# Row maxima of a two-head side: both heads in the two halves of TensorE's array, from the high parts alone, with VectorE adding the masks

## The reference, cut to what matters

```python
def _attn(q, k, v, mask=None):
    s = jnp.einsum('bhqd,bhkd->bhqk', q, k) / np.float32(np.sqrt(HD))
    if mask is not None:
        s = jnp.where(mask, s, jnp.float32(-1000000000.0))
    return jnp.einsum('bhqk,bhkd->bhqd', jax.nn.softmax(s, -1), v)
...
o1 = _attn(q, k1, v1, causal[None, None])
...
o2 = _attn(q, ks, vs)
...
winmask = causal & (ii[:, None] - ii[None, :] < WINDOW)
o3 = _attn(q, kw, vw, winmask[None, None])
```

## Time and profile before

| | |
|---|---|
| three runs, us | 3157.45, 3162.90, 3165.65 (median 3162.9) |
| the profiled execution, us | 3156.08 |
| its span, us | 3154.3 |
| mean granted TensorE clock | 0.923 of full |
| busy share over the span | TensorE matmul 86%, VectorE 58%, ScalarE 44%, GpSimd 20% |
| TensorE busy in the slices of the attention part | nine tenths or more in nearly all |

### The profile page before, as it was taken

The page is one execution under the profiler, slowest core; times in us unless marked ns, Lnnn a source line. Parts: engine busy times, 40 slices in busy tenths (PEclk is TensorE's granted clock), DMA queues, the critical chain, the costliest instruction groups (busy, mean ns, idle before and its releaser), DMA issues. The chain is left out here.

```text
span 3154.3 us, 48599 instructions
## 1 busy us (share of the span) xinstructions
PE 2699.1 (86%) x17280; PEld 1719.6 (55%) x17280; DVE 1818.9 (58%) x3117; ACT 1373.8 (44%) x2816; POOL 634.7 (20%) x607
## 2 busy tenths in 40 slices
PE   5666575763999997999997999998999994999999
PEld 3544344442555554555654655554555552777777
DVE  4746656484466555456555556655646644667655
ACT  2333233230444543544543545543545453555544
POOL 0322405042011001001101001101101102445445
PEclk9787878785999998999998999999999996999999
DMA  2542617068655464555554455654554512000000
GB/s 85 196 159 104 251 47 304 24 246 218 127 107 120 108 124 96 114 125 120 108 114 106 106 121 114 130 115 96 124 116 98 121 33 87 18 17 3 20 10 7
DMA packets 191886, 342.32 MB, mean 109 GB/s; under 512 B 65632, under 2 KB 95040, under 8 KB 191152
## 3 DMA queue, kind: packets, MB, share of 16 engines
q1 hardware_dynamic: 191664, 339.49, 42.6%
HBM read 224.56 MB, written 112.99 MB: 107 GB/s over the span
## 5 line engine op out<-in xcount | busy, mean ns | idle before, releaser
L1340 ACT ACTIVATE prob<-ps 128x512 f32<-128x512 f32 (+5 forms) x1600 | 645.2, 441 | 903.1 <-PE ps L1291 828.3
L1393 DVE TENSOR_REDUCE maxima<-ps 128x1 f32<-128x512 f32 (+3 forms) x768 | 387.4, 547 | 352.3 <-PE ps L1222 181.3
L1312 PE MATMUL ps<-prob,plain 128*32 128x512 f32 (+5 forms) x3200 | 587.5, 449 | 0.0
L1363 POOL TENSOR_TENSOR products<-products,sums 128x256 f32<-128x256 f32 x192 | 140.5, 732 | 1695.2 <-DVE sums L1384 1694.0
L1398 DVE TENSOR_REDUCE maxima<-ps 128x2 f32<-128x512 f32 (+1 forms) x512 | 297.5, 611 | 271.4 <-PE ps L1240 129.9
L1384 DVE RECIPROCAL sums<-sums 128x256 f32<-128x256 f32 x192 | 331.6, 1736 | 96.8 <-ACT sums L1351 96.8
L1312 PE MATMUL ps<-prob,v_s 128*32 128x512 f32 (+3 forms) x1536 | 316.3, 497 | 0.0
L1283 PE MATMUL ps<-q1a_s,k1a_s 128*128 128x512 f32 (+3 forms) x768 | 307.6, 401 | 0.0
L1291 PE MATMUL ps<-q1b_s,k1b_s 128*128 128x512 f32 (+3 forms) x768 | 301.9, 394 | 0.0
L1668 POOL TENSOR_TENSOR hl<-hid,hh 128x512 fp32r<-128x512 f32 x176 | 228.5, 1298 | 262.6 <-ACT hh L1612 258.2
L1283 PEld LDWEIGHTS ps<-q1a_s,k1a_s 128*128 128x128 f32 x768 | 144.8, 188 | 233.0 <-ACT prob L1340 161.5
(11 more groups left out here) (300 smaller groups left out, 5591.4 us busy)
## 6 DMA issues: line engine op xcount, KB each, us to landing
qh_dram<-pairs SPq DMA_DIRECT2D x96, 512.0 KB, 3.6
kwh_dram<-pairs SPq DMA_DIRECT2D x64, 512.0 KB, 2.7
qa_s<-qh_dram SPq DMA_DIRECT2D x128, 256.0 KB, 4.6
kwa_s<-kwh_dram SPq DMA_DIRECT2D x128, 256.0 KB, 7.5
q1a_s<-qh_dram SPq DMA_DIRECT2D x128, 256.0 KB, 4.7
qb_s<-qh_dram SPq DMA_DIRECT2D x64, 256.0 KB, 9.0
kwb_s<-kwh_dram SPq DMA_DIRECT2D x64, 256.0 KB, 10.0
k1a_s<-k1ah_dram SPq DMA_DIRECT2D x32, 512.0 KB, 6.9
```

The source lines that it names most:

```text
L1312: mm = pe.matmul(ps[at:at + VD, SCORES + k % 2, q0 - c * CH:q0 - c * CH + w], w_, m.prob[:, n % PROBS, h, 0:w], start=first, stop=True, sk ...
L1340: act.activation(m.prob[:, u % PROBS, h, 0:w], ps[:, turn % SCORES, 0:w], ACT.Exp, scale=SCALE).then_inc(s["exp_done"], 1)
L1363: pool.tensor_tensor(o, o, m.sums[:, br, cc], ALU.mult).then_inc(s["divided"], 1)
L1393: ins = dve.tensor_reduce(partial[:, h, i, part:part + 1], bank[:, 0:w], AX, ALU.max)
```

## The change

Each maxima fill now makes both heads, each in a bank of its own (`fills` lists such a step twice, `banks` is 2). Head 0 uses rows 0 to 63 of the array, head 1 rows 64 to 127, each with 64 rows: the high parts of the queries against those of the keys. To that end the loads put head 1's low parts above its high parts (`upper_and_lower`), which takes one DMA for a head and part: 8 in place of 4 for `qa` and for `q1a`. The exact pass is unchanged. The low parts of the queries no longer enter a maximum. The mask matmuls are gone: VectorE adds the masks, now fp32 in SBUF, in a `tensor_tensor_reduce` of the masked columns (the last 128 of a tile in `max0`, each 192 of `max2`), and reduces the unmasked columns of `max0` by themselves into a third place of `partial`. The list of `preparation` has 20 maxima steps of two banks instead of 40 of one.

```diff
-    max0 = [("max0", side, h, i, part) for h in range(HP) for i in range(NT) for part in range(1 + (i >= NT // 2))]
-    max1, max2 = [[(kind, side, h, k) for h in range(HP) for k in range(NT // 2)] for kind in ("max1", "max2")]
-    todo = max2 + max1[:3] + [("rows", side, 2)] + max1[3:] + max0[:3] + [("rows", side, 1)] + max0[3:]
+    max0 = [("max0", side, i, part) for i in range(NT) for part in range(1 + (i >= NT // 2))]
+    max1, max2 = [[(kind, side, k) for k in range(NT // 2)] for kind in ("max1", "max2")]
+    todo = max2 + max1[:2] + [("rows", side, 2)] + max1[2:] + max0[:2] + [("rows", side, 1)] + max0[2:]
...
-        self.fills = self.of(("max0", "max1", "max2", "rows", "proj"))
+        self.fills = [x for x in steps if x[0] in ("rows", "proj")
+                      or x[0] in ("max0", "max1", "max2") for h in range(HP if x[0][:3] == "max" else 1)]
...
+    def upper_and_lower(first):
+
+        return [(h, at, comp + (lo ^ h)) for h in range(HP) for lo in range(2)
+                for at, comp in ((64 * lo, first), (64 * lo + 32, 4))]
...
-                for at, comp in ((0, 2), (32, 4), (64, 3), (96, 5)):
-                    sp.dma_start(m.qa[at:at + 32, k].bitcast(F32), two(src.q[g, comp], side)).then_inc(near, 16)
+                for h, at, comp in upper_and_lower(2):
+                    sp.dma_start(m.qa[at:at + 32, k, h].bitcast(F32), one(src.q[g, comp], side, h)).then_inc(near, 16)
...
-                if n >= SPARES:
-                    pe.wait_ge(s["emptied"], n - SPARES + 1)
-                bank, k = ps[:, 8 - SPARES + n % SPARES, :], side % 2
+                def bank(h):
+                    if n + h >= SPARES:
+                        pe.wait_ge(s["emptied"], n + h - SPARES + 1)
+                    return ps[:, 8 - SPARES + (n + h) % SPARES, :]
+
+                k = side % 2
+                upper = [slice(HD * h, HD * h + HD) for h in range(HP)]
                 if kind == "max0":
-                    h, i, part = a
+                    i, part = a
...
-                    mm = pe.matmul(bank[:, 0:k1 - k0], m.q1a[:, k, h, i * P:(i + 1) * P],
-                                   m.k1a[:, k, k0:k1], start=True, stop=True)
-                    if k1 == (i + 1) * P:
-                        mm = pe.matmul(bank[:, k1 - k0 - P:k1 - k0], m.ident_bf[:], m.causal_q[:],
-                                       start=False, stop=True, skip_group_check=True)
+                    for h, r in enumerate(upper):
+                        pe.matmul(bank(h)[:, 0:k1 - k0], m.q1a[r, k, h, i * P:(i + 1) * P], m.k1a[r, k, k0:k1],
+                                  start=True, stop=True).then_inc(s["fill_ready"], 1)
                 elif kind == "max1":
...
+                    both = [bank(h) for h in range(HP)]
                     for i in range(2):
-                        t = 2 * pair + i
-                        mm = pe.matmul(bank[:, i * KEEP:(i + 1) * KEEP], m.qa[:, k, h, t * P:(t + 1) * P],
-                                       m.ksa[:, k, h, :], start=True, stop=True)
+                        t = 2 * a[0] + i
+                        for h, r in enumerate(upper):
+                            mm = pe.matmul(both[h][:, i * KEEP:(i + 1) * KEEP], m.qa[r, k, h, t * P:(t + 1) * P],
+                                           m.ksa[r, k, h, :], start=True, stop=True, skip_group_check=True)
+                            if i == 1:
+                                mm.then_inc(s["fill_ready"], 1)
...
+                        rest = w if (i >= NT // 2 and part == 0) else w - P
+                        if rest > 0:
+                            ins = dve.tensor_reduce(partial[:, h, i, part:part + 1], bank[:, 0:rest], AX, ALU.max)
+                        if rest < w:
+                            ins = dve.tensor_tensor_reduce(bank[:, rest:w], bank[:, rest:w], m.causal_q[:], 1.0,
+                                                           LOWEST, ALU.add, ALU.max, partial[:, h, i, 2:3])
+                        ins.then_inc(s["emptied"], 1)
...
+                    elif kind == "max2":
+                        for i in range(2):
+                            t = 2 * step[2] + i
+                            ins = dve.tensor_tensor_reduce(
+                                bank[:, i * KEEP:i * KEEP + WN], bank[:, i * KEEP:i * KEEP + WN],
+                                m.window_q0[:] if t == 0 else m.window_q[:], 1.0, LOWEST, ALU.add, ALU.max,
+                                negs[2][:, h * NT + t:h * NT + t + 1])
+                        ins.then_inc(s["emptied"], 1)
```

More of the change, by code:

```diff
@@ L1006, in count, with banks @@
         return self.of((step[0],)).index(step) + 1
+    def banks(self, step):
+        return 2 if step[0][:3] == "max" else 1
     def loaded(self, which, side):
@@ L1156, in whole @@
                 far, late = s["far%d" % k], s["late%d" % k]
-                for at, comp in ((0, 0), (32, 4), (64, 1), (96, 5)):
-                    sp.dma_start(m.q1a[at:at + 32, k].bitcast(F32), two(src.q[g, comp], side)).then_inc(far, 16)
+                for h, at, comp in upper_and_lower(0):
+                    sp.dma_start(m.q1a[at:at + 32, k, h].bitcast(F32), one(src.q[g, comp], side, h)).then_inc(far, 16)
                 sp.dma_start(m.k1a[:, k].bitcast(F32), src.k1a).then_inc(far, 16)
@@ L1232, in fill @@
                 elif kind == "max2":
-                    h, pair = a
                     once("near%d" % k, 16 * NEAR * plan.loaded("local", side))
+                    both = [bank(h) for h in range(HP)]
                     for i in range(2):
-                        t = 2 * pair + i
+                        t = 2 * a[0] + i
                         k0 = max(0, t * P - WINDOW)
-                        pe.matmul(bank[:, i * KEEP:i * KEEP + WN], m.qa[:, k, h, t * P:(t + 1) * P],
-                                  m.kwa[:, k, h, k0:k0 + WN], start=True, stop=True, skip_group_check=True)
-                        mm = pe.matmul(bank[:, i * KEEP:i * KEEP + WN], m.ident_bf[:],
-                                       m.window_q0[:] if t == 0 else m.window_q[:], start=False, stop=True,
-                                       skip_group_check=True)
+                        for h, r in enumerate(upper):
+                            mm = pe.matmul(both[h][:, i * KEEP:i * KEEP + WN], m.qa[r, k, h, t * P:(t + 1) * P],
+                                           m.kwa[r, k, h, k0:k0 + WN], start=True, stop=True, skip_group_check=True)
+                            if i == 1:
+                                mm.then_inc(s["fill_ready"], 1)
@@ L1253, in fill @@
                     pe.wait_ge(s["o_done"], PIECES * (NC * g + c + 1))
-                    pe.matmul(bank, m.wvp[:, g], m.products[:, 0, cc], start=True, stop=False)
-                    mm = pe.matmul(bank, m.wproj[:, g], m.products[:, 1, cc], start=False, stop=True)
-                mm.then_inc(s["fill_ready"], 1)
+                    pe.matmul(bank(0), m.wvp[:, g], m.products[:, 0, cc], start=True, stop=False)
+                    pe.matmul(ps[:, 8 - SPARES + n % SPARES, :], m.wproj[:, g], m.products[:, 1, cc], start=False,
+                              stop=True).then_inc(s["fill_ready"], 1)
             def scores(side, u):
@@ L1323, in _ @@
                     fill(n, *step)
-                    n += 1
+                    n += plan.banks(step)
         @block.scalar
@@ L1403, in _ @@
+                if kind[:3] == "max":
+                    continue
+                if kind == "rows":
                     br = step[2]
@@ L1405, in _ @@
                         dve.wait_ge(s["rows%d" % br], 16 * plan.nth(side))
-                    ins = dve.tensor_copy(m.mrows[:, br, :].bitcast(F32R), bank[0:HP * NT, 0:P])
+                    ins = dve.tensor_scalar(m.mrows[:, br, :].bitcast(F32R), bank[0:HP * NT, 0:P], -1.0, None, ALU.mult)
                 else:
```

50 lines of the change are left out of this document (24 added, 26 removed).

## The result

The changed kernel takes **3264.1 us** (median of 4 runs, 3261.7 to 3271.8) against 3162.7 for the kernel before (3157.5 to 3165.7): ratio 1.033, interval 1.030 to 1.035. Forecast were 3229, between 3130 and 3300. The sign and the kind of the loss were right, the size was short by 35 us, and the forecast's own range, 3195 to 3265, ends 1 us above the result. The profiled execution has a span of 3260.0 us.

The account below looks back on a forecast made before the run. TensorE's matmul stream was taken to bound the attention part. Fills, double-unit stops and VectorE chains gave +1.9 us a side, 59 us over 31 windows, plus 7 for the opening: 3229 us, range 3130 to 3300, own range 3195 to 3265.

Parts of the forecast that it names:

- the four double units: Four units a window with two pairs need four banks, so TensorE waits for VectorE to empty one: 3.8 us a side.
- VectorE's chain: Maxima pairs queue on VectorE with the reciprocals: 2.4 us lost on even sides, 2.7 on odd, mean 2.5 a side.
- a turn: TensorE switching between full-array and half-array matmuls: 0.09 us, with the open weight load 0.20 an entry, 16 entries a side.
- The fills: TensorE's matmuls filling banks for the maxima: 11.5 us a side before, 7.0 after with entries, if nothing stops them.
- The masked maximum: VectorE's masked reduction: 0.26 and 0.08 us for the read at 128 columns, 0.33 and 0.08 at 192.
- The opening: Start of the kernel: 3.5 us more for query DMAs and some 3.5 more VectorE work, together 7 us.
- 7.0 + 3.8 + 2.5 - 11.5: Per side: fills after, double-unit stops and VectorE's chains, less fills before: +1.8 us, 1.9 unrounded, 59 us over 31 windows.
- The stop of 1.5 us before the third kept-key pair: On odd sides two reciprocals stand between kept-key pairs 2 and 3 on VectorE, costing 1.5 us.
- Free turns: Rival: the step between 128 and 64 rows costs nothing, 3.2 us a side go, 3130 us; chance 0.16.
- Halves that load one after the other: Rival: the second half's weights wait for the first's, 2.6 us a side, 81 us, 3310 us; chance 0.10.
- The masked maximum at twice the price: Rival: 0.13 and 0.20 us more on masked maxima in chains and double units, 2.1 us a side, 3294; chance 0.09.
- Nothing to measure: Rival: the double units' stops are partly made up by shorter later waits, kernel stays near 3163 us; chance 0.08.

Follow-up runs that it names:

- experiment 7: Changed kernel with each reciprocal over 32 of its 256 columns only, the rest of the sums left uninverted: 3126.6 us, 0.990 of the kernel before.
- experiment 9: Kernel before with only the projections moved two units of scores later: 3138.1 us, 0.992 of the kernel before.
- experiment 11: Changed kernel with one pair in a unit, reciprocals over 32 of 256 columns and projections two units later: 3038.9 us, 0.962 of the kernel before.
- experiment 3: Changed kernel with the masks left out of the maxima, one plain VectorE reduction a bank: 3240.9 us, 1.025 of the kernel before.
- experiment 6: Changed kernel with two unread matmuls ahead of every projection's wait and two ahead of even sides' third kept-key pair: 3214.7 us, 1.018 of the kernel before.
- experiment 12: Changed kernel, complete, steps reordered (one a unit in even passes, a table in odd ones), projections two units later: 3094.9 us, 0.979 of the kernel before.
- experiment 8: Changed kernel with every projection but the last two units of scores later: 3208.7 us, 1.015 of the kernel before.
- experiment 4: Kernel before with only the masks moved to VectorE's masked maximum, fills single and full-array, no mask matmul: 3117.3 us, 0.987 of the kernel before.
- experiment 2: Changed kernel with preparation steps spread evenly over the 25 units, so no unit has two pairs: 3284.0 us, 1.039 of the kernel before.
- experiment 10: Kernel before with masks added on VectorE and every projection but the last two units later: 3064.4 us, 0.970 of the kernel before.
- experiment 5: Changed kernel with eight unread matmuls ahead of every projection's wait and six ahead of even sides' third kept-key pair: 3398.8 us, 1.075 of the kernel before.

## Why the prediction was right, and where it was not

**Right in kind.** TensorE's stream bounds the part, the four double units stop it, VectorE's chain holds the pairs back, and the halves work beside each other at the price of a turn. At the full clock I had +1.9 us a side and the passes show +1.6. So the forecast's own mechanism gives 49 us where I had put 66. That the measured time still lies inside my narrower range is luck: 56 us of the clock, which were in no term, took the place of what was too much there, and more. These terms were off, and partly cancelled:
- *The fills.* With short reciprocals after (54.8, experiment 7) and no wait for the projection before (54.6 and 55.0, experiment 9), the fills and their stops cost the same before and after: 0.0 a side, where 7.0 + 3.8 - 11.5 gives -0.7. The stops were not the cause: one pair in a unit saves 54.8 - 51.75 = 3.0 us (experiments 7 and 11) net of four more entries at 0.20, 0.8 together, so they are worth the 3.8 of the forecast. The matmuls beside each other were right too: from start to start the 20 pairs of experiment 11 take 7.8 us, which is 3.8 and, for each pair, 0.20 for the open load and the way out. What was too small was the turn. In an even pass the second score matmuls with the turn behind them take 12.43 us after and 10.58 before, 0.115 for each of 16 entries where I had 0.09; that is 0.4 of the 0.7. The three transposes take 0.44 for 0.27, which was in no term. The last 0.1 is a difference of several small ones that I did not separate.
- *VectorE's chains.* 2.0 and 2.7 us are what the reciprocals cost after; but the kernel before already paid 0.5 and 1.0 in front of the projections. Net 1.6, where I had put down 2.5. For the odd pass I had summed the new waits and subtracted no old one.
- *The masked maximum.* I took 0.34 and 0.41 us with the read. In a row it costs 0.21 to 0.25 and 0.32. Leaving the masks out still gives 0.7 us a side: the list of waits then has 10 us less between the pairs of branch 0 and 8 less in front of the projections (experiment 3).
- *The opening.* I had +7 us; the first pass starts at 793.5 us after and at 795.8 before, which is nothing.

**Missing: the clock.** "Sum. 7.0 + 3.8 + 2.5 - 11.5" took every row at the full clock and priced a stop at its own length. The stop of 1.5 us before the third kept-key pair was forecast, and measured it is 1.48 us of idle time. What I did not ask is what TensorE's clock does behind it. The two views of one odd pass, TensorE's timeline and the windows around the stop:

```profile
1365.90 0.34 PE L1311 MATMUL ps<-qb_s,kwb_s 128*128 128x192 f32 x1
1367.71 0.50 PE L1248 MATMUL ps<-ksa_s,qa_s 64*128 64x256 f32 x4 [1.48 <-DVE maxima L1423]
```

```profile
1360.00:1365.90 5.90, 5.90 (x52) 3.34 (x51) 5.12 (x6) 4.60 (x10) 2.28 (x4) 1.00 0.02 5
1366.20:1367.70 1.50, 0.04 (x1) 0.02 (x1) 1.50 (x3) 0.40 (x2) 0.94 (x2) 1.00 0.00 0
1369.00:1382.50 13.50, 13.37 (x65) 6.81 (x65) 7.06 (x16) 4.66 (x10) 2.31 (x4) 0.50 0.29 71
```

Before the stop the engine was busy without a gap, in it 0.04 of 1.5 us, and from 1368.8 on the clock is 0.50, 1.2 GHz, for 13.7 us. The pass loses 1.5 us in the stop and 5.7 behind it. Behind a projection's wait of 2.2 us (2.22 idle) the even pass has 3.4 us of low clock, which costs 1.5. The Trainium skill (TensorE: Matmul & The Clock Gate, A second HAM failure mode: psum-queue depth-cycling) describes another kernel, in which short idle times between groups of matmuls that cycle through PSUM banks make the clock swing, and puts the loss on the swing between bursts. By experiment 6 (49 us back with no stop shortened) and by the 5.7 us behind a stop of 1.5 this trace agrees. The kernel before had the sign of it too, its low clock at the three borders between batches, each behind stops; I read 0.98 as "full" and did not look where the 0.02 lay.

**The rivals.** Free turns: no, 0.10 us. Halves that load one after the other: no, where both banks are free the heads' matmuls start 3 to 4 ns apart; only in the three double units of branch 0 does the second head of the second pair run alone. The masked maximum at twice the price: no, it is cheaper than assumed. Nothing to measure: no; but in a better order the same instructions are faster than before (experiment 12).

What stays open is why the same stop lowers the clock in one pass and not in the next. The stop of 1.48 us does it in 5 of the 12 odd passes away from the borders after, and in 10 of 12 in experiment 8. The projection's wait does it in 9 of 12 even passes of experiment 4 (1.78 us idle) and in none of experiment 2 (1.83 idle). So which stop will cost more than its own length can't be forecast from its length alone.

## What to carry to other kernels

A stop of one or two microseconds in an otherwise dense stream of matmuls can cost several times its length (here 1.5 us, and 5.7 behind it): for each such stop, look at the granted clock of the microseconds behind it, and add what the passes with the low clock take more. Where an order is fixed by hand and fills share few banks, count the banks that a unit needs and what VectorE has queued ahead of them; here the order alone was worth 169 us, and matmuls that nobody reads won 49. And take a change of two ideas apart: the masks on VectorE gain 42 us (experiment 4), the pairs on the two halves lose 147 on top of that in the order in which they were made, and 30 in the best order tried (experiments 12 and 10).

## What the hardware showed that I had not expected

- The clock can fall behind stops of 1.0 to 2.2 us (1.02 in two odd passes of experiment 4, 1.48 and 2.22 after), and inside a pass stays low for 3.4, 6.8, 10.2 or 13.7 us, though TensorE was busy in 13.37 of 13.50 us of such a stretch. After a stop that is filled it didn't fall (experiments 5 and 6).
- Two matmuls on the two halves of the array, entered pair by pair, cost what two full-array matmuls in a row do (51.7 us a pass either way).
- The accumulator's read of a masked maximum takes 0.14 us in the list, but the next operation starts 0.2 to 0.3 us after the one before it, so that it costs nearly nothing in a row.
